# Three of sixteen state products of a selective scan moved from VectorE to GpSimd, in the first five of its eight batches

## The reference, cut to what matters

```
dA    = exp(delta[e, t] * A[e, n])
state = state * dA + delta[e, t] * u[e, t] * B[n, t]        # a recurrence in t, one per (e, n)
y[e, t] = sum over n of state[e, n, t] * C[n, t]
y = (y + D[e] * u) * silu(z)
```

## Time and profile before

| | us |
|---|---|
| median of three executions | 2397.37 (2394.19 to 2400.5) |
| the profiled execution | 2404.08 |
| its span, first to last instruction | 2402.1 |
| scan stage, first to last scan | 150.6 to 1411.3 |
| groups 0 to 19, the ones that change | 150.6 to 944.1 |

### The profile page before, as it was taken

The page is one execution under the profiler, slowest core; times in us unless marked ns, Lnnn a source line. Parts: engine busy times, 40 slices in busy tenths (PEclk is TensorE's granted clock), DMA queues, the critical chain, the costliest instruction groups (busy, mean ns, idle before and its releaser), DMA issues. The chain is left out here.

```text
span 2402.1 us, 18775 instructions
## 1 busy us (share of the span) xinstructions
PE 1959.0 (82%) x5107; PEld 901.3 (38%) x5107; DVE 1415.0 (59%) x1962; ACT 855.9 (36%) x1392; POOL 989.3 (41%) x889
## 2 busy tenths in 40 slices
PE   8837678788787795599999973889599999999990
PEld 2212233233233341144444432445255555555540
DVE  6869988888887878797888844654010111111113
ACT  5545545364544444555656420110011111111110
POOL 0057766666575665887777731211400000000005
PEclk9968889899898997799999985999799999999995
DMA  5044354302203004368687645211654555455536
GB/s 185 22 194 105 140 110 107 112 5 99 89 8 153 1 14 155 138 225 339 224 305 277 215 153 189 68 50 58 242 179 152 180 180 166 160 179 180 175 123 214
DMA packets 100992, 352.50 MB, mean 147 GB/s; under 512 B 15200, under 2 KB 15200, under 8 KB 82464
## 3 DMA queue, kind: packets, MB, share of 16 engines
q1 hardware_dynamic: 93216, 326.21, 39.7%
q0 software_dynamic: 7680, 25.17, 3.1%
HBM read 288.29 MB, written 63.05 MB: 146 GB/s over the span
## 5 line engine op out<-in xcount | busy, mean ns | idle before, releaser
L561 POOL TENSOR_TENSOR work<-work,big 128x512 f32<-128x512 f32 x512 | 658.5, 1291 | 265.7 <-DVE bank L608 263.9
L474 PE MATMUL bank<-work,ident 128*128 128x512 f32 x928 | 536.9, 693 | 226.5 <-DVE work L592 175.9
L608 DVE TENSOR_TENSOR_SCAN bank<-bank,work 128x512 f32<-128x512 f32 x512 | 624.9, 1221 | 137.5 <-ACT bank L528 88.9
L528 ACT ACTIVATE bank<-work,An 128x512 f32<-128x512 f32 x512 | 345.9, 691 | 256.2 <-DVE work L592 253.1
L474 PEld LDWEIGHTS bank<-work,ident 128*128 128x128 f32 x928 | 179.5, 216 | 521.6 <-DVE work L592 333.7
L592 DVE TENSOR_TENSOR work<-bank,big 128x512 f32<-128x512 f32 x512 | 343.9, 672 | 9.1 <-PE bank L474 8.8
L1655 POOL DMA_INDIRECT W<-ys_d,slot x32 | 33.9, 1059 | 644.4 <-PEq L1642 634.9
L1612 PE MATMUL bank<-Y,big 128*128 128x512 f32 x528 | 263.6, 596 | 0.0
L1195 DVE SCALAR_TENSOR_TENSOR work<-work,bank 128x352 f32<-128x352 f32 (+1 forms) x63 | 36.6, 581 | 329.0 <-ACT work L1185 328.9
L957 PE MATMUL bank<-W,work 128*128 128x512 f32 x384 | 198.6, 622 | 0.0
L1173 ACT COPY work<-bank 128x512 f32<-128x512 f32 x63 | 36.9, 585 | 396.9 <-PE bank L1158 396.9
(11 more groups left out here) (249 smaller groups left out, 2252.8 us busy)
## 6 DMA issues: line engine op xcount, KB each, us to landing
big<-bc_d SPq DMA_DIRECT2D x64, 1024.0 KB, 6.7
work<-gate SPq DMA_DIRECT2D x39, 704.0 KB, 4.2
work<-up SPq DMA_DIRECT2D x39, 704.0 KB, 4.1
W<-gate SPq DMA_DIRECT2D x24, 1024.0 KB, 4.9
W<-up SPq DMA_DIRECT2D x24, 1024.0 KB, 5.5
W<-down SPq DMA_DIRECT2D x24, 1024.0 KB, 5.4
work<-down SPq DMA_DIRECT2D x39, 512.0 KB, 3.8
work<-xs_d SPq DMA_DIRECT2D x63, 256.0 KB, 4.4
```

The lines of the kernel that those rows point to most:

```text
L474: nc.tensor.matmul(YS[:, :], ident[:, :], hC[ring(g * NS + u[0])], start=v == 0, stop=v == len(units[g]) - 1).then_inc(sum_done, 1)
L528: nc.scalar.activation(H[i % 4][:, :], delta[g % 2], ACT.Exp, scale=An[vb // B][:, g % NJ, i:i + 1]).then_inc(dA_done, 1)
L561: nc.gpsimd.tensor_tensor(dBu[i % 2], du[g % 2], Bb[:, i, :], ALU.mult).then_inc(dBu_done, 1)
L608: nc.vector.tensor_tensor_scan(H[i % 4][:, :], H[i % 4][:, :], dBu[i % 2], 0.0, ALU.mult, ALU.add).then_inc(scan_done, 1)
```

## The change

States 4, 8 and 12 of each of groups 0 to 19 are "lent": their scan writes to the SBUF tile hC and not back into the PSUM bank, VectorE leaves their product out, and GpSimd multiplies the tile by C in place, after its dBu of step 6, 10 or 15. The waits move with it. The lent scan now waits for its tile to be free (it was the product that waited). ScalarE's dA four states later waits for the lent scan and not for a product. The sum of a lent state stands one step after GpSimd's multiplication, and the sums behind it stay behind it.

```diff
+            LENT = {4: 2, 8: 2, 12: 3}
+            def lent(s):
+                return not paired(s // NS) and s % NS in LENT
...
-                return max(u[-1] + (3 if len(u) == 2 else 1), when(g, v - 1) if v else y_at[g] + 2)
+                return max(u[-1] + (3 if len(u) == 2 else LENT[u[0]] + 1 if lent(g * NS + u[0]) else 1), when(g, v - 1) if v else y_at[g] + 2)
...
-                        pe.wait_ge(hC_done, g * NS + u[0] + 1)
+                        product(pe, g * NS + u[0])
...
-                    at_least(act, hC_done, s - 3)
+                    if s >= 4 and lent(s - 4):
+                        act.wait_ge(scan_done, s - 3)
+                    elif s >= 4:
+                        product(act, s - 4)
...
+                    for i0 in LENT:
+                        if i0 + LENT[i0] == i and lent(g * NS + i0):
+                            s0 = g * NS + i0
+                            if g % NJ == 0:
+                                pool.wait_ge(C_in[i0 // 4], (vb + 1) * 16)
+                            pool.wait_ge(scan_done, s0 + 1)
+                            nc.gpsimd.tensor_tensor(hC[ring(s0)], hC[ring(s0)], Cb[:, i0, :], ALU.mult).then_inc(pool_hC, 1)
...
+                if lent(s):
+                    return
                 dve.wait_ge(scan_done, s + 1)
+                ring_free(dve, s)
+                nc.vector.tensor_tensor(hC[ring(s)], H[i % 4][:, :], Cb[:, i, :], ALU.mult).then_inc(hC_done, 1)
...
+                    if lent(s):
+                        ring_free(dve, s)
+                    nc.vector.tensor_tensor_scan(hC[ring(s)] if lent(s) else H[i % 4][:, :], H[i % 4][:, :], dBu[i % 2], 0.0,
                                                  ALU.mult, ALU.add).then_inc(scan_done, 1)
```

More of the change, by code:

```diff
@@ L375, in scan_stage @@
             sum_done, y_done, picked, pool_added, sq_done = (sem("s_" + a) for a in ("sum_done", "y_done", "picked", "pair_added", "square_done"))
+            pool_hC = sem("s_pool_hC_done")
             dt1_in, u1_in, zeroed = sem("s_dt1_in"), [sem(f"s_u1_in{b}") for b in range(B)], sem("s_zeroed")
@@ L407, in when, with product @@
                 u = units[g][v]
-                return max(u[-1] + (3 if len(u) == 2 else 1), when(g, v - 1) if v else y_at[g] + 2)
+                return max(u[-1] + (3 if len(u) == 2 else LENT[u[0]] + 1 if lent(g * NS + u[0]) else 1), when(g, v - 1) if v else y_at[g] + 2)
+            LENT = {4: 2, 8: 2, 12: 3}
+            def lent(s):
+                return not paired(s // NS) and s % NS in LENT
+            own0 = [0]
+            for s_ in range(GROUPS * NS):
+                own0.append(own0[-1] + (not lent(s_)))
+            def product(eng, s):
+                if lent(s):
+                    eng.wait_ge(pool_hC, s + 1 - own0[s + 1])
+                else:
+                    eng.wait_ge(hC_done, own0[s + 1])
             def steps():
@@ L435, in loads @@
                         sp.wait_ge(dBu_done, g * NS + i + 1)
-                        sp.wait_ge(hC_done, g * NS + i + 1)
+                        sp.wait_ge(hC_done, own0[g * NS + i + 1])
+                        at_least(sp, pool_hC, g * NS + i + 1 - own0[g * NS + i + 1])
                         chunk(vb + 1, i // 4)
                     if vb < 2 and n == 20:
-                        sp.wait_ge(hC_done, g * NS + i)
+                        sp.wait_ge(scan_done, g * NS + i)
                         zeros(vb)
@@ L568, in gpsimd @@
                             pool_du(pool, g + 1)
+                    for i0 in LENT:
[5 more added lines that the diff above has]
+                            nc.gpsimd.tensor_tensor(hC[ring(s0)], hC[ring(s0)], Cb[:, i0, :], ALU.mult).then_inc(pool_hC, 1)
                     if (i - 3, i - 2) in pairs[g]:
-                        pool.wait_ge(hC_done, s - 1)
+                        product(pool, s - 2)
                         nc.gpsimd.tensor_tensor(hC[ring(s - 3)], hC[ring(s - 3)], hC[ring(s - 2)], ALU.add).then_inc(pool_added, 1)
@@ L581, in dve_hC, with ring_free @@
                     dve.wait_ge(C_in[i // 4], (g // NJ + 1) * 16)
+                if lent(s):
+                    return
                 dve.wait_ge(scan_done, s + 1)
+                ring_free(dve, s)
+                nc.vector.tensor_tensor(hC[ring(s)], H[i % 4][:, :], Cb[:, i, :], ALU.mult).then_inc(hC_done, 1)
+            def ring_free(dve, s):
                 was = next((s - d for d in range(1, min(s, NS) + 1) if ring(s - d) == ring(s)), None)
@@ L591, in dve_hC @@
                     side.past(dve, "vtr_done", B * NJ)
-                nc.vector.tensor_tensor(hC[ring(s)], H[i % 4][:, :], Cb[:, i, :], ALU.mult).then_inc(hC_done, 1)
             def dve_y(dve, g):
@@ L607, in vector @@
                     dve.wait_ge(dBu_done, s + 1)
-                    nc.vector.tensor_tensor_scan(H[i % 4][:, :], H[i % 4][:, :], dBu[i % 2], 0.0,
+                    if lent(s):
+                        ring_free(dve, s)
+                    nc.vector.tensor_tensor_scan(hC[ring(s)] if lent(s) else H[i % 4][:, :], H[i % 4][:, :], dBu[i % 2], 0.0,
                                                  ALU.mult, ALU.add).then_inc(scan_done, 1)
```

## The result

The changed kernel takes 2418.05 us, the median of four executions (2414.45 to 2427.08), against 2398.09 us for the kernel before, timed beside it on the same chip. The ratio is 1.009 with an interval of 1.0059 to 1.0121. It is slower by 20 us, where the forecast was 21.6 more, 2419 us.

A forecast was written before the change was run, and what follows sets the result against it. VectorE looked like the bound but was often held by ScalarE, GpSimd and TensorE, with GpSimd nearly the bound in batch 0. 9.2 + 9.9 + 2.5 = 21.6 us on the median 2397.4 gives 2419; 8-in-10 range 2396 to 2440.

The forecast's parts named there:

- Batch 0: Groups 0 to 3: 1.9 us from GpSimd's added work plus 0.4 from scan 4's wait, 2.3 a group, 9.2 in all.
- delay y by 0.8 more: Batch 0, upper bound only: sums 12 to 15 all wait for product 12 and may make y 0.8 us later.
- The wait that moves: Batch 0: scan 4 now waits for sum 1 and starts 2.6 us later; part is hidden, scan 7 0.4 us late.
- Batches 1 to 3: Followed group by group in batch 2: 3.3 us longer per batch, 9.9 for three, bounds 1 and 5 per batch.
- batch 4: Longer waits for ScalarE and routing work: 2.5 us longer, bounds 0 and 5.
- all three products saved lie under transfer waits: Fourth group of a batch: it runs from transfer to transfer, product 12 costs nothing, 3.3 us carry into the next batch.
- takes up all but 0.6: Third group of batch 2: y's earlier 3.84 us wait for TensorE absorbs the 1.8 us delay except 0.6.
- After group 20: Batches 5 to 7 and after: only the start moves, the delay reaches the end in full, time the same within 2 us.
- The lower terms, 5 + 3 + 0: Lower bounds in us for batch 0, batches 1 to 3 and batch 4, used for the forecast's own range, 2407 to 2430.
- the first: Rival: VectorE's saving comes through in batches 1 to 4, 12 us gained after a small batch 0 loss, 2385; chance 0.12.
- The third: Rival: four sums at step 0 make y late in batches 1 to 4 too, 41 us slower, 2438; chance 0.12.
- The fourth: Rival: lent scans writing SBUF share with GpSimd and slow by 0.7 us each, about 2450; chance 0.04.

The follow-up runs named there:

- own_tile3: The change, but the lent states write to a fourth SBUF tile of their own (third shared-expert matrix not loaded, second used instead): 2395.91 us, ratio 0.9994.
- no_mult: The change with GpSimd's 60 multiplications by C left out, TensorE's sums waiting for the scan instead: 2399.05 us, ratio 1.0006.
- own_no_mult: The change with both a fourth tile for lent states (third shared-expert matrix not loaded) and GpSimd's multiplications left out: 2379.59 us, ratio 0.9921.
- change_late: The change with all three states lent in batches 1 to 4 only, not batch 0: 2407.49 us, ratio 1.004.
- before_no_down: The kernel before, with only layer 0's third shared-expert matrix not loaded and the second used instead: 2401.80 us against 2399.60, ratio 1.0008.
- The square: Four medians against the kernel before: the change +20.0 us, without GpSimd's multiplications +1.3, with an own tile for lent states -2.3, with both -19.6.

## Why the prediction was right, point by point

The sign, the size and the two mechanisms held. That the total came within 2 us was in part luck: in batches 1 to 4 the prediction left out a gain and a cost of about 20 us each, and these cancelled. By its own steps, in the profile (shift of a start against the kernel before):

- **Batch 0: 9.2 forecast, 11.5 measured** (2.4, 2.9, 3.2 and 2.9 for the groups). From scan 7 of a group to the next scan 0, GpSimd's chain cost 1.4 to 1.6 us where I took 1.9 (bounds 1.25 and 1.92). It has no idle time from dBu 9 to dBu 0, as forecast, but it grew by 2.04 us (18.06 less 16.02) and not by 2.46, so 0.42 of the 0.67 us in which it had waited for the pick were used after all. By scan 7 in group 2 the moved wait cost nothing, not 0.4, since it lay whole under the wait for dA; in group 0 it left 1.0 us there, about what own_tile3 gives back in batch 0 (1.2). What was missing is the item that I had only in the upper bound, at 0.8 us: the sums bunch behind product 12. They do it at step 0 through the ring of tiles: product 15 waits for sum 13 and stands ahead of y, so y is late, and 1.4 to 1.6 us a group come of it in groups 1 to 3. The step sized wrong is "delay y by 0.8 more", left out of the middle value. That GpSimd's time carries batch 0 is shown by no_mult (3.8) and own_no_mult (0.6); change_late puts the whole of it at 11.6 us of the median.
- **The wait that moves.** In batch 0 lent scans waited 2.44 us in group 0 and 1.23 in the other three, not 2 or more each: the rest of the lateness had been paid at product 15 already. The waits for dBu rose by 17.8 us (15 or more was forecast).
- **Batches 1 to 3: 9.9 forecast, 8.5 measured; batch 4: 2.5 forecast, 5.4 measured.** With the scatter that before_no_down shows these sums can't be told from the forecast, and change_late, which is the change in these batches alone, has 8.4 in the median against 12.4 forecast (interval 5 to 14). Their make-up can be told, and it is wrong in two places. The first is the saving. For the fourth group of a batch the forecast had "all three products saved lie under transfer waits", and in the other three it counted no saving either, without a reason. With both costs away own_no_mult gains 19.6 us of the median, and as its batch 0 stays at 0.6, this lies in batches 1 to 4 (VectorE's saving is at most 48 x 0.59 = 28 us there). The second is the moved wait, which the forecast had cost little: with product 12 it came to 3.3 us a batch. The square gives the moved wait alone 21 to 22 us, of which the profiles put 1.2 in batch 0 (3.2 without the multiplications), so 4 to 5 us a batch. GpSimd's work cost 8 to 11 us in batches 1 to 4 (17 to 19, less 8 to 10 in batch 0). So a gain of some 20 us and a cost of some 20 us were not counted or counted small, and they cancel. That the total is right there is luck.
- **One of these waits in detail.** Scan 8 of the second group was to wait 0.9 us for sum 5. It waited 2.44. VectorE and TensorE of the changed kernel at that place:

```profile
514.56 1.22 DVE L644 TENSOR_TENSOR_SCAN work<-bank,work 128x512 f32<-128x512 f32 x1 [2.44 <-PE bank L493]
```

```profile
506.14 2.08 PE L493 MATMUL bank<-work,ident 128*128 128x512 f32 x2 [1.64 <-DVE work L615]
508.01 1.69 PE L993 MATMUL bank<-W,work 128*128 128x512 f32 x2
...
512.54 2.74 PE L493 MATMUL bank<-work,ident 128*128 128x512 f32 x6
```

TensorE's order was as I read it, but it came out of an idle time at half pace (2.08 us for two matmuls) and reached sums 4 and 5 late. The half pace of the first two rows costs 0.95 and 0.67 us against 1.13 and 1.02 at full pace, 1.6 in all, and the wait is 1.5 longer than forecast. The granted clock was 0.55 over these two rows (506.14 to 509.70 us) and 1.00 after them. I had priced only the order. By groups, the forecast had 1.8, 1.9 and 3.3 us at the starts of the third and fourth group and of the next batch; measured from the start of batch 2 they are 4.3, 2.5 and 2.9.
- **The third group's y "takes up all but 0.6".** The starts of groups 9 and 10 are 13.5 and 17.7 us late, that of group 11 15.8, so 1.9 us were taken up. But the 3.84 us that I counted on belong to the one profiled execution; in another of the same order it is 0.80. Over groups 0 to 19 y waited 12.0 us for TensorE in the one and 6.0 in the other, and 1.1 in the changed kernel.
- **After group 20.** Its start is 25.3 us late, and this stays within 0.4 us to the last scan, as forecast. Behind the stage 2.9 us come back; nothing there was changed. So the time after group 20 is 2.5 us shorter, a little outside the 2 us that I gave it, and within what two executions of one order differ by (3.0, by before_no_down).
- **A sum in the range.** The lower terms, 5 + 3 + 0, give 2397.4 + 8 = 2405, and not the 2407 that stands there. The result lies inside either.
- **Lent scans are not slower.** 1197 to 1225 ns, median 1212, against 1222 for those that write PSUM:

```profile
L644 DVE TENSOR_TENSOR_SCAN work<-bank,work x60: 1197/1212/1225, 159.5 to 954.8; 128x512 f32<-128x512 f32 x60
```

The Trainium skill (SBUF — State Buffer, Who interferes with whom) says that a VectorE instruction with at most one SBUF input, outside the 2-port modes, doesn't contend with GpSimd. This row agrees: beside a GpSimd busy for 115.18 of 139.80 us in batch 0, no lent scan took over 1225 ns.

Of the rivals, the first had the right mechanism in the wrong company: in batches 1 to 4 a gain is there, and with one state and hardly a wait before it, it comes through. The third, that the sums bunch, is what batch 0 shows in part. The fourth, slower lent scans, is ruled out by the row above.

## What to carry to other kernels

When work moves to another engine, list each wait that the old instruction carried and ask which instruction carries it now and what is queued behind that: here the wait for a tile, two instructions earlier in line, cost as much as GpSimd's added work. Move only the pieces whose wait is long over, where the new engine has room, and try them one at a time; state 8 alone, outside batch 0, gained 17 us, and all three states in all five batches lost 20. And take a second profile of the same kernel before a single wait is counted on as cover.

## What the runs showed of the hardware

- The same two matmuls, after the same idle time of 1.41 us and in the same instruction order, took 2.08 us in one execution, at a granted clock of 0.50, and 1.13 in another, at 1.00 (1.2 and 2.4 GHz). A wait of VectorE behind them went from 3.84 to 0.80 us. Over batches 1 to 4 two executions of one order differ by 7 us, while batch 0 repeats within 0.3.
- VectorE's pick, all in SBUF, ranged from 716 to 2466 ns beside a busier GpSimd (724 to 2459 before), with a lower median. GpSimd's multiplication in place took 1250 to 1721 ns:

```profile
L597 POOL TENSOR_TENSOR work<-work,big x60: 1250/1266/1721, 162.1 to 963.3; 128x512 f32<-128x512 f32 x60
```

So a product costs 1.23 us back to back on GpSimd and 0.59 on VectorE, twice as much for each one moved.
